# A fused transformer block on one core: TensorE's attention bodies without a loop, and the next block of x turned between the items of the projection

## What is computed

```python
mod = silu(condition) @ Wada + bada                 # (8, 6*512)
sh_a, sc_a, gt_a, sh_m, sc_m, gt_m = split(mod, 6)
xn = layernorm(x, g1, be1)                          # x: (8, 1024, 512) fp32
xm = xn * (1 + sc_a) + sh_a
x  = x + gt_a * attention(xm, Wqkv, Wproj, bproj)   # 16 heads of 32, causal
xn = layernorm(x, g2, be2)
xm = xn * (1 + sc_m) + sh_m
x  = x + gt_m * (gelu(xm @ W1 + b1) @ W2 + b2)      # hidden width 2048
```

## Time and profile before

| what | value |
|---|---|
| median of the runs | 3539.05 us (3533.94 to 3541.70) |
| the profiled execution's own time | 3540.59 us |
| its span, first to last instruction | 3538.9 us |
| mean granted TensorE clock | 0.967 |
| TensorE matmul busy | 3307.9 us, 93% |
| VectorE, GpSimd, ScalarE busy | 56%, 41%, 33% |
| attention stage, setup included | 0 to about 1800 us |

### The profile page before, as it was taken

One profiled execution on the slowest core, in us unless ns is written; L12 is line 12 of the kernel. 1 busy time (PEld: TensorE's weight loads), 2 busy tenths in 40 slices (PEclk: granted clock), 3 DMA queues, 4 the chain that ended last, 5 costly groups with the idle time before them and its releaser, 6 DMA issues.

```text
span 3538.9 us, 72400 instructions
## 1 busy us (share of the span) xinstructions
PE 3307.9 (93%) x25708; PEld 2624.5 (74%) x25708; DVE 1995.6 (56%) x2415; ACT 1173.1 (33%) x2322; POOL 1443.8 (41%) x1200
## 2 busy tenths in 40 slices
PE   7889899999999999998857999999999999999999
PEld 4656666666666666665536999989998999899898
DVE  4555666655665556656626555555555555555552
ACT  2135445444455444545541111111111111111111
POOL 3235455445555444555555233333323333333232
PEclk9989999999999999999988999999999999999999
DMA  5545555455555555555542222222222222212220
GB/s 204 172 132 158 152 159 175 147 157 156 149 175 159 150 154 157 162 162 155 159 125 64 58 71 57 65 56 71 50 63 64 60 61 56 71 50 69 59 59 13
DMA packets 303549, 392.47 MB, mean 111 GB/s; under 512 B 24240, under 2 KB 206000, under 8 KB 303336
## 3 DMA queue, kind: packets, MB, share of 16 engines
q1 hardware_dynamic: 289904, 367.84, 36.0%
q10 hardware_dynamic: 13440, 21.50, 1.7%
HBM read 270.66 MB, written 118.06 MB: 110 GB/s over the span
## 4 chain that ended last, share of the span: by engine, by line
PE 86%; DVE 7%; issue 3%; ACT 2%; DMA 1%; POOL 0%; SPq 0%; ACTq 0%; DVEq 0%
PE psH L800 21%; PE psY L813 20%; PE psA L623 10%; PE psT L662 7%; PE psA L700 6%; PE psA L619 5%; PE psP L779 5%; PE psS L637 4%; DVE mx L1100 3%; PE psA L673 3%; PE psA L708 2%; DVE psS L1096 2%; ACT e L882 1%; PE psP L789 1%; PE psA L602 1%
## 5 line engine op out<-in xcount | busy, mean ns | idle before, releaser
L1339 POOL TENSOR_TENSOR h_l<-h_full,h_h 128x256 fp32r<-128x256 f32 x512 | 489.4, 956 | 1120.5 <-DVE h_h L1259 1120.5
L882 ACT ACTIVATE e<-psT 128x512 f32<-128x512 f32 (+1 forms) x1202 | 608.5, 555 | 743.5 <-PE psT L662 739.7
L1100 DVE TENSOR_REDUCE mx<-psS 128x4 f32<-128x2048 f32 (+3 forms) x384 | 666.6, 1757 | 238.7 <-PE psS L637 233.2
L979 ACT ACTIVATE h_full<-psH,b1c 128x256 f32<-128x256 f32 x512 | 244.0, 477 | 1332.3 <-PE psH L800 1332.3
L1376 POOL TENSOR_TENSOR es<-e 128x1024 f32<-128x1024 f32 x192 | 458.1, 2386 | 511.9 <-ACT e L882 375.9
L800 PE MATMUL psH<-a_h,w1p_h 128*128 128x256 f32 x2048 | 578.0, 282 | 7.5 <-DVE a_l L1254 7.5
L800 PE MATMUL psH<-a_h,w1p_l 128*128 128x256 f32 x2048 | 580.4, 283 | 0.0
L800 PE MATMUL psH<-a_l,w1p_h 128*128 128x256 f32 x2048 | 580.0, 283 | 0.0
L662 PEld LDWEIGHTS psT<-qst,kst 97*128 97x128 f32 x2404 | 360.1, 195 | 199.2 <-issue 123.3
L662 PE MATMUL psT<-qst,kst 97*128 97x256 f32 (+1 forms) x2404 | 438.7, 300 | 66.3 <-issue 41.1
L1259 DVE CAST h_h<-h_full 128x256 fp32r<-128x256 f32 x512 | 148.4, 290 | 542.9 <-ACT h_full L979 541.6
(11 more groups left out here) (109 smaller groups left out, 4764.9 us busy)
## 6 DMA issues: line engine op xcount, KB each, us to landing
qk_split<-qk_hl SPq DMA_DIRECT2D x128, 512.0 KB, 3.3
kst<-qk_split SPq DMA_DIRECT2D x128, 256.0 KB, 3.7
qst<-qk_split SPq DMA_DIRECT2D x128, 256.0 KB, 3.9
xin<-in_x_dram SPq DMA_DIRECT2D x64, 256.0 KB, 3.7
values<-vout ACTq DMA_DIRECT2D x64, 256.0 KB, 2.3
kmx<-qk_split SPq DMA_DIRECT2D x32, 512.0 KB, 4.7
qmx<-qk_split SPq DMA_DIRECT2D x32, 512.0 KB, 5.3
kst<-qk_split SPq DMA_DIRECT2D x128, 128.0 KB, 3.5
```

What stands on the lines that cost most here:

```text
L882: act.activation(e[:, s % ERING, 2 * hp:2 * hp + 2, 0:w], score_bank(s, hp, with_a)[:, :, 0:w], ACT.Exp, scale=SCALE).then_inc(sem("exp_do ...
L979: act.activation(h_full[:, m % 4, :], psH[:, m % 4, 0:RA], ACT.Gelu, bias=b1c[:, m:m + 1])\
L1100: reduce = dve.tensor_reduce(mx[:, part, :, qt], psS[:, :, col:col + w], AX_X, ALU.max)
L1339: return pool.tensor_tensor(dst, full, high.bitcast(F32), ALU.subtract)
```

## The change

TensorE's stream has bodies 0 to 15 written out one after another; the other four engines keep their loops. The xm tile is gone: a turned and modulated quarter is written back over the columns of xin it came from, and the splits read it there. The shares are spread to 36 steps, so the items end at steps 2, 5, 8, ... 35; turns stand at steps 21, 27, 33 and 36, after items 6, 8, 10 and 11, in the same bank. The load of x, its statistics and its normalisation move to earlier steps, the splits one step earlier. Turns and items get counters of their own (`a_turned`, `a_modulated` beside `a_formed`, `a_copied`). Block 3's turns in the setup use two banks.

```diff
-A_SHARES = ((6, 0, 6), (2, 8, 2), (8, 4)) * 4
+A_SHARES = ((6, 0, 6), (2, 8, 2)) * 6
-TURN_AT = (34, 35, 36, 37)
-SPLIT_HI_AT, SPLIT_LO_AT = 38, 39
-LOAD_X_AT = (5, 7, 9, 11)
-LN_STATS_AT, LN_AGGR_AT, LN_NORM_AT = (14, 16, 18, 20), 22, (26, 28, 30, 32)
+TURN_AT, TURN_AFTER = (21, 27, 33, 36), (7, 9, 11, 12)
+SPLIT_HI_AT, SPLIT_LO_AT = 37, 38
+LOAD_X_AT = (1, 2, 3, 4)
+LN_STATS_AT, LN_AGGR_AT, LN_NORM_AT = (6, 8, 10, 12), 13, (16, 17, 18, 20)
...
-        xm, xm_l = sb_full_low(att, "xm", [P, KT, XB])
+        xm_l = sb(att, "xm_l", [P, KT, XB], F32R)
...
+        def modulated(ia, k):
+            return normalised(ia).rearrange("p r (k c) -> p k r c", k=KT)[:, k]
+        def by_rows(t):
+            return t.rearrange("p k (r c) -> p k r c", c=P)
...
-                        sp.wait_ge(sem("a_formed"), (ia - 1) * A_N + A_TURNS)
+                        sp.wait_ge(sem("xm_lo"), ia)
+                        past(sp, "sp")
+                        sp.wait_ge(sem("xm_lo_pool"), ia)
...
-                wait(pe, sem("a_copied"), ia * A_N + k - int(alone))
+                if not alone:
+                    pe.wait_ge(sem("a_copied"), (ia - 1) * A_ITEMS + TURN_AFTER[k])
+                elif k < 2:
+                    wait(pe, sem("a_copied"), (ia - 1) * A_ITEMS + A_ITEMS - 1 + k)
+                else:
+                    pe.wait_ge(sem("a_modulated"), ia * A_TURNS + k - 1)
...
-                    wait(pe, sem("a_copied"), ia * A_N + A_TURNS + n - int(alone))
+                    if alone and n < 2:
+                        pe.wait_ge(sem("a_modulated"), ia * A_TURNS + A_TURNS - 1 + n)
+                    elif turns and n in TURN_AFTER:
+                        pe.wait_ge(sem("a_modulated"), (ia + 1) * A_TURNS + TURN_AFTER.index(n) + 1)
+                    else:
+                        pe.wait_ge(sem("a_copied"), ia * A_ITEMS + n - int(alone))
...
             for k in range(A_TURNS):
-                a_turn(AHEAD, k, False)
+                a_turn(AHEAD, k, True)
             body(0, True, True)
-            with pe.Fori(1, NU - AHEAD - 1) as u:
+            for u in range(1, NU - AHEAD - 1):
                 body(u, True, True)
             body(NU - AHEAD - 1, True, False)
-            with pe.Fori(NU - AHEAD, NU - 1) as u:
+            for u in range(NU - AHEAD, NU):
                 body(u, False, False)
-            body(NU - 1, False, False)
...
-                dve.wait_ge(sem("a_copied"), ia * A_N + A_TURNS)
-                wait(dve, sem("a_formed"), ia * A_N)
-                dve.tensor_copy(xm_h[:], xm[:]).then_inc(sem("xm_hi"), 1)
+                dve.wait_ge(sem("a_modulated"), ia * A_TURNS + A_TURNS)
+                wait(dve, sem("a_formed"), ia * A_ITEMS)
+                dve.tensor_copy(by_rows(xm_h[:]), modulated(ia, slice(0, KT))).then_inc(sem("xm_hi"), 1)
```

More of the change, by code:

```diff
@@ L36 @@
 A_ITEMS = A_NV + A_NQK
-A_N = A_TURNS + A_ITEMS
 A_MM = 12
-A_SHARES = ((6, 0, 6), (2, 8, 2), (8, 4)) * 4
+A_SHARES = ((6, 0, 6), (2, 8, 2)) * 6
 A_STORE_LAG = 2
@@ L454, in load_piece @@
                 n = (u - PIECE_BODY) * 4 + q
-                sp.wait_ge(sem("a_formed"), NXB * A_N)
+                sp.wait_ge(sem("a_formed"), NXB * A_ITEMS)
                 if isinstance(u, int) and u == NU - 1:
@@ L599, in a_turn, with a_item @@
                     pe.wait_ge(sem("xn_ready"), ia + 1)
-                wait(pe, sem("a_copied"), ia * A_N + k - int(alone))
+                if not alone:
[4 more added lines that the diff above has]
+                    pe.wait_ge(sem("a_modulated"), ia * A_TURNS + k - 1)
                 for r in range(NXR):
                     mm = pe.transpose(psA[:, bank, r * P:(r + 1) * P], normalised(ia)[:, r, k * P:(k + 1) * P], ident[:])
-                mm.then_inc(sem("a_formed"), 1)
-            def a_item(ia, n, first, end, alone):
+                mm.then_inc(sem("a_turned"), 1)
+            def a_item(ia, n, first, end, alone, turns):
                 bank = n % 2 if alone else 1
@@ L723, in body @@
                     if at and not late:
-                        a_item(u + AHEAD, *at, False)
+                        a_item(u + AHEAD, *at, False, with_ln)
                     if r == MAX_TURN_AT and not (last and h == 1):
@@ L747, in _ @@
                 for n in range(A_ITEMS):
-                    a_item(ia, n, 0, A_MM, True)
+                    a_item(ia, n, 0, A_MM, True, False)
                     if ia == AHEAD - 1:
@@ L856, in a_modulate @@
                 b = ia // 2
-                act.wait_ge(sem("a_formed"), ia * A_N + k + 1)
+                act.wait_ge(sem("a_turned"), ia * A_TURNS + k + 1)
                 ca, cb = (coef[:, w, b, k:k + 1] if isinstance(ia, int) else
                           coef[:, w, bass.ds(b, 1), k] for w in (0, 1))
-                act.activation(xm[:, k, :], psA[:, k % 2 if alone else 1, :], ACT.Identity, scale=ca, bias=cb)\
-                   .then_inc(sem("a_copied"), 1)
+                act.activation(modulated(ia, k), psA[:, k % 2 if alone else 1, :].rearrange("p (r c) -> p r c", c=P),
+                               ACT.Identity, scale=ca, bias=cb).then_inc(sem("a_modulated"), 1)
             def a_copy(ia, n, alone):
@@ L871, in a_copy @@
                     dst, src = qk_hl[:, m % QK_RING, LOW[m // IPB]], psA[:, n % 2 if alone else 1, :]
-                act.wait_ge(sem("a_formed"), ia * A_N + A_TURNS + n + 1)
+                act.wait_ge(sem("a_formed"), ia * A_ITEMS + n + 1)
                 act.activation(dst, src, ACT.Copy).then_inc(sem("a_copied"), 1)
@@ L898, in v_store @@
             def v_store(ia, n):
-                act.wait_ge(sem("a_copied"), ia * A_N + A_TURNS + n + 1)
+                act.wait_ge(sem("a_copied"), ia * A_ITEMS + n + 1)
                 past(act, "act")
@@ L944, in _ @@
             for k in range(A_TURNS):
-                a_modulate(AHEAD, k, False)
+                a_modulate(AHEAD, k, True)
             body(0, True, True, 0)
@@ L1053, in normalise @@
                 dve.wait_ge(sem("ln_rstd"), ia + 1)
-                wait(dve, sem("a_formed"), ia * A_N - A_ITEMS)
+                if isinstance(ia, int) and 0 < ia <= AHEAD:
+                    dve.wait_ge(sem("xm_lo_pool"), ia)
+                    past(dve, "dve")
+                    dve.wait_ge(sem("xm_lo"), ia)
                 a = dve.tensor_scalar(normalised(ia)[:, r], xin[:, r], aggr[:, r, 0:1], rstd[:, r:r + 1],
@@ L1074, in a_split_low @@
                 dve.wait_ge(sem("xm_hi"), ia + 1)
-                dve.tensor_tensor(xm_l[:, k], xm[:, k], xm_h[:, k].bitcast(F32), ALU.subtract)\
+                dve.tensor_tensor(by_rows(xm_l[:, k]), modulated(ia, k), by_rows(xm_h[:, k].bitcast(F32)), ALU.subtract)\
                    .then_inc(sem("xm_lo"), 1)
@@ L1081, in a_high @@
                     m = n - A_NV
-                    dve.wait_ge(sem("a_copied"), ia * A_N + A_TURNS + n + 1)
+                    dve.wait_ge(sem("a_copied"), ia * A_ITEMS + n + 1)
                     dve.tensor_copy(qk_hl[:, m % QK_RING, HIGH[m // IPB]].bitcast(F32R),
@@ L1347, in a_split @@
                 pool.wait_ge(sem("xm_hi"), ia + 1)
-                low(xm_l[:, 0:KT // 2], xm[:, 0:KT // 2], xm_h[:, 0:KT // 2]).then_inc(sem("xm_lo_pool"), 1)
+                k = slice(0, KT // 2)
+                low(by_rows(xm_l[:, k]), modulated(ia, k), by_rows(xm_h[:, k])).then_inc(sem("xm_lo_pool"), 1)
             def a_low(ia, n):
```

## The result

The changed kernel takes 3450.68 us (median of four runs, 3448.68 to 3451.37) against 3540.38 us for the kernel before on the same chip: a ratio of 0.9746, 95% interval 0.9729 to 0.9764, or 90 us less. The forecast was 3462 us, the range 3448 to 3492.

What follows compares the result with a forecast made beforehand. TensorE was taken as the bound, waiting at its loop jumps. The terms 47.0 + 15 + 5 - 3 + 10 + 3 = 77 us off the profiled 3540.6 gave 3463.6, forecast as 3462 us; range 3448 to 3492.

Steps and rivals of the forecast that it cites:

- Two of its signs: Attention stage: no wait of an item for xm_l at a border; no TensorE "issue" wait over 1 us.
- (1): TensorE's loop jumps between bodies: writing out removes ten of 4.18 us and one of 5.2 us, 47.0 us.
- The register rows: TensorE's stream: some 190 register rows a body leave it, not costed.
- (2): Body borders 0 to 11: splits a step earlier remove item 0's wait for xm_l, 12 x 1.25 = 15 us.
- The 1.3 us to spare: Body border: GpSimd's half of xm_l ends at 1491.8, item 0 wants it at 1493.1.
- (3): Turns among the items: turn waits balance out; half of the exponent waits, at step 32, go, 5 us gained.
- (4): VectorE in steps 16 to 20: normalisations between maxima delay the turn by 0.3 us a body, 3 us lost.
- the balance: Turns in a body: 10.2 us of old waits for ScalarE against three new waits of about 0.35 us, nothing gained.
- (5): Clock dips near the end of bodies: spreading items and turns gains 0 to 20 us, taken as 10 us.
- (6): Setup: two banks for block 3's turns remove three waits of 0.87 us for ScalarE, 3 us.
- the dips go as well: Rival for the bodies' clock dips: parts 1, 2, 3 and the whole clock gain, 3452 us; chance 0.17.
- The figure of the Trainium skill: TensorE's instruction memory holds 2048 instructions, so bodies 13 and 14's loop should fit; by it the sum is 5 us smaller.

Runs made afterwards that it cites:

- VectorE's half late: Changed kernel with VectorE's half of xm_l made after the last maxima again (step 39), GpSimd's half left at step 38: 3490.67 us, ratio 0.9854.
- quarter on GpSimd: Changed kernel with three quarters of xm_l made by VectorE and one by GpSimd: 3443.66 us, ratio 0.9731.
- low part early: Kernel before with TensorE's bodies written out and xm_l made straight behind the high part, three quarters by VectorE: 3476.44 us, ratio 0.9821.

## Why the prediction was right, and where it was not

The time was inside the range and the main cause is the one forecast, but that the sum came within 13 us is in part luck: three of its terms were off by more than that.

- **The cause, right.** TensorE's stream was the bound, the jumps were the place to look, straight code costs nothing and the other engines' loops don't show. Writing out alone makes the kernel faster, 26 us. Two of its signs did not come: item 0 still waits for xm_l, and an "issue" wait of 1.6 us is left, which is that one.
- **(1) The jumps, mis-sized.** "A jump costs 4.18 us" came from two periods without one, both with a slow stretch ahead of item 0 that hid part of its wait. The step that failed is "what is late next is in the two periods without a jump already". Ten written-out periods have 105.6 us in the mean, not 103.85. Measured: 26 us for 47 on its own. In the new places a jump is worth 4.9 us a period. The register rows that left, which were not costed, are 164 in a looped body, not 190.
- **(2) The splits, wrong in the mechanism and too low in size.** The wait of item 0 was to go; it stayed at 1.57 us, because GpSimd's subtraction takes 3.40 us beside VectorE's. The row for this was in the setup of the trace of before, where VectorE's half runs beside it too, and I took the duration of a body's end, where VectorE read from PSUM. The 1.3 us to spare were wrong too. They were read at a border with a slow stretch, where item 0 was wanted 4.9 us after the cast began; at the full-speed border above it was wanted after 3.2 us (1213.74 - 1.57 - 1208.95). With 2.37 us GpSimd's half would still have come some 0.5 us late, an estimate from these rows. Yet making xm_l sooner was worth 38 us, not 15, since it shortened waits of 2.9 us which had half clock behind them.
- **(3) and (4) Turns, exponents and normalisations, right in the main**: half of the exponent's waits gone, 0.3 us at turn 0 in ten of ten periods, 0.3 us a turn. But two turns of a body wait for a copy, not three, so the balance is 10.2 less 5.8, a gain of 4.4 us in ten periods, not nothing; and the wait for the maxima's turn, 4.1 us, was left out.
- **(5) The clock, right in sign, far too small, and by another cause.** I priced only the dip near step 38, 10 us, and gave it to the spread of items and turns. Over the ten periods the time at half clock fell from 92.2 to 20.5 us, which is up to 36 us of full-speed work. Writing out and the early low part alone bring it to the same 20.5, so with the low part early the spread had no part in it that shows; what went are stretches at the jumps and behind long waits.
- **(6) The setup, right** in direction: the first item of body 0 comes at 201.9 us in place of 205.6, 3.8 us sooner for 3.
- **The sum** was 77 us, measured 90. Errors in both directions met: 21 too much in (1) taken alone, 34 too little in the rest. Of the rivals, "the dips go as well" (3452 us) has the time to within 2 us, and that is luck: its 20 us for the clock are too few, its 47 and 15 for (1) and (2) not what these parts gave, and every border still has a dip or a wait.
- The figure of the Trainium skill (Runtime: NRT & Kernel Launch, "Instruction fetch mechanics") by which the jump of bodies 13 and 14 should cost nothing was rightly passed over: in the trace of before it left TensorE idle for 4.2 us, and the period that held it gave 8.0 us, in part by the clock.

## What to carry to other kernels

A wait that lies under another wait has no row of its own. Before you price the removal of one, list what else is due at that place and when each comes, and see whether the two or three samples of the place without it are all of one kind. Look at the granted clock around each sample: here a slow stretch made a border look cheap, and made the room behind the cast look larger than it is. When two engines split a piece of work that both read from SBUF, take the duration of each from a moment when they run together.

## What the runs showed of the hardware that was not expected

- A wait of TensorE of 2.9 us at a border was followed by half clock for 3.4 or 6.8 us each time, 12 of 12 in the run with VectorE's half late and 5 of 5 in the one written out alone, and so such a border cost 3.1 us more than one of the changed kernel (12 periods, 36.8 us). Of eight waits of 1.57 us in the changed kernel three were followed by half clock; of those of 1.0 us (quarter on GpSimd, six) and 1.3 us (low part early, five) none.
- GpSimd's subtraction makes next to no headway while VectorE subtracts from SBUF, some 0.15 us' worth: 1024 columns take 2.37 us alone and 3.40 beside 1.23 us of VectorE's; 512 take 1.28 alone and 2.84 beside 1.76.
- TensorE's jump back takes 0.21 us for a pass of some 1280 matmuls and weight loads, 3.6 to 5.0 us for one of some 1600 (bodies 13 and 14, three runs), 3.8 to 6.0 us for one of some 1930 (bodies 1 to 11) and 3.6 to 5.1 us for one of 2560; it doesn't grow further for a pass of two attention bodies (4.3 to 4.6 us).
